# Moving lags of a causal convolution between VectorE and TensorE around the first layer norm

## The reference, cut to what matters

```
x = x + conv(x, cond)             # causal, per channel, 32 taps: y[b,t,c] = sum_j cond[31-j,c] * x[b,t-j,c]
ada = cond @ ada_w + ada_b        # shift1, scale1, gate1, shift2, scale2, gate2, one row per batch
x1  = ln(x) * (1 + scale1) + shift1
qkv = x1 @ qkv_w + qkv_b          # 16 heads of 128; attention inside each batch of 32 tokens
y   = x + gate1 * (softmax(q k / sqrt(128)) v @ out_w + out_b)
x2  = ln(y) * (1 + scale2) + shift2
out = x + (y + gate2 * (gelu(x2 @ ffn_w1 + ffn_b1) @ ffn_w2 + ffn_b2))
```

## Time and profile before

| what | value |
|---|---|
| median of 3 runs | 314.86 us (313.95 to 314.98) |
| the profiled execution's own time | 313.68 us |
| its span | 311.9 us |
| busy: PE, DVE, ACT, POOL | 96%, 56%, 55%, 39% of the span |
| granted TensorE clock | 0.999 of full speed over the span |

### The profile page before, as it was taken

One profiled execution on the slowest core, in us unless ns is written; L12 is line 12 of the kernel. 1 busy time (PEld: TensorE's weight loads), 2 busy tenths in 40 slices (PEclk: granted clock), 3 DMA queues, 4 the chain that ended last, 5 costly groups with the idle time before them and its releaser, 6 DMA issues.

```text
span 311.9 us, 6134 instructions
## 1 busy us (share of the span) xinstructions
PE 300.7 (96%) x2604; PEld 252.0 (81%) x2604; DVE 173.3 (56%) x297; ACT 171.3 (55%) x309; POOL 120.4 (39%) x103
## 2 busy tenths in 40 slices
PE   4978999999999999999999999999999999999995
PEld 3875997878898878788887888888898888688885
DVE  3997698987865635472535554440620556555232
ACT  5752567534762745486365736644762794713901
POOL 5007819331820634072337214531911571611400
PEclk9999999999999999999999999999999999999999
DMA  7902322400250070007004300520160020000012
GB/s 245 361 11 86 112 76 65 141 0 2 72 200 0 2 259 14 0 4 269 1 2 154 117 2 2 183 89 2 39 230 2 2 67 0 3 0 0 2 67 68
DMA packets 15259, 23.00 MB, mean 74 GB/s; under 512 B 792, under 2 KB 8320, under 8 KB 15232
## 3 DMA queue, kind: packets, MB, share of 16 engines
q1 hardware_dynamic: 15184, 22.58, 21.4%
q10 hardware_dynamic: 48, 0.03, 0.0%
HBM read 21.57 MB, written 1.05 MB: 73 GB/s over the span
## 4 chain that ended last, share of the span: by engine, by line
PE 85%; DVE 9%; POOL 3%; DMA 1%; ACT 1%; issue 1%; DVEq 0%; POOLq 0%
PE bank L914 18%; PE bank L916 18%; PE bank L915 18%; PE bank L988 9%; DVE xc L536 6%; PE bank L922 5%; PE bank L923 4%; PE bank L924 4%; PE bank L972 3%; POOL wl L292 3%; PE bank L869 2%; PE bank L894 1%; DMA crow<-in_cond_dram 1%; DVE yacc L667 1%; PE bank L846 1%
## 5 line engine op out<-in xcount | busy, mean ns | idle before, releaser
L292 POOL TENSOR_TENSOR wl<-raw,wh 128x512 fp32r<-128x512 f32 x72 | 98.7, 1398 | 133.2 <-ACT wh L355 116.5
L401 ACT ACTIVATE pool<-bank,bT 128x512 f32<-128x512 f32 x56 | 38.5, 688 | 57.0 <-PE bank L916 57.0
L914 PE MATMUL bank<-x1h,wl 128*128 128x512 f32 (+1 forms) x176 | 67.6, 384 | 0.8 <-DVE x1l L605 0.4
L916 PE MATMUL bank<-x1h,wh 128*128 128x512 f32 (+1 forms) x176 | 65.2, 370 | 0.0
L915 PE MATMUL bank<-x1l,wh 128*128 128x512 f32 (+1 forms) x176 | 65.1, 370 | 0.0
L653 DVE SCALAR_TENSOR_TENSOR ol<-bank,bT,oh 128x512 fp32r<-128x512 f32 x32 | 24.0, 749 | 36.7 <-ACT oh L426 35.7
L536 DVE SCALAR_TENSOR_TENSOR xc<-x,condT,xc 128x496 f32<-128x496 f32 (+27 forms) x82 | 42.8, 592 | 0.1
L355 ACT ACTIVATE wh<-raw 128x512 fp32r<-128x512 f32 x72 | 40.9, 622 | 3.5 <-PE bank L916 3.5
L914 PEld LDWEIGHTS bank<-x1h,wl 128*128 128x128 f32 x176 | 33.2, 189 | 7.8 <-DVE x1l L605 0.8
L915 PEld LDWEIGHTS bank<-x1l,wh 128*128 128x128 f32 x176 | 33.2, 189 | 6.0 <-issue 0.7
L916 PEld LDWEIGHTS bank<-x1h,wh 128*128 128x128 f32 x176 | 33.1, 188 | 5.8
(11 more groups left out here) (114 smaller groups left out, 412.8 us busy)
## 6 DMA issues: line engine op xcount, KB each, us to landing
raw<-in_L_cond_qkv_w_dram SPq DMA_DIRECT2D x24, 512.0 KB, 5.7
raw<-in_L_cond_out_w_dram SPq DMA_DIRECT2D x8, 512.0 KB, 3.6
raw<-in_L_cond_ffn_w_dram SPq DMA_DIRECT2D x4, 512.0 KB, 5.0
adaw<-in_L_cond_ada_w_dram SPq DMA_DIRECT2D x1, 1024.0 KB, 10.7
out_dram<-pool SPq DMA_DIRECT2D x3, 256.0 KB, 2.2
pool<-in_x_dram SPq DMA_DIRECT2D x2, 256.0 KB, 3.2
adaw<-in_L_cond_ada_w_dram SPq DMA_DIRECT2D x1, 512.0 KB, 5.2
pool<-in_x_dram SPq DMA_DIRECT2D x1, 512.0 KB, 6.1
```

Source lines behind the costliest of these rows:

```text
L292: g.tensor_tensor(wl[:, cols], raw[:, cols], wh[:, cols].bitcast(F32), ALU.subtract)\
L401: a.activation((q_sb if j < GH else k_sb)[:, j % GH, :], src, ACT.Identity, bias=bias(U, j // GH, j % GH)).then_inc(s_ev, 1)
L914: pe.matmul(dst, wl[:, w_cols], a_hi, start=start, stop=False)
L916: return pe.matmul(dst, wh[:, w_cols], a_hi, start=False, stop=stop)
```

## The change

VectorE takes all 16 lags 0 to 15 for the first quarter, but of the second quarter only lag 0 at first. TensorE takes lags 16 to 31 for the whole of half 0. The second quarter's lags 8 to 15 go to TensorE (`conv(1, ...)`, 256 tokens wide, into the banks `OB`) between the steps of `norm` 0; its lags 1 to 7 go to VectorE, one lag behind `centre(0)`, two behind `var_eps(0)`, four behind `x1_low(0)`. Then `conv_sum_second_quarter` adds the bank. Half 1 gets no lag on TensorE: VectorE does all 32 (`conv(2, ...)`), and its sum goes. There are 48 diagonals instead of 36 (GpSimd 16 instead of 9, ScalarE 32 instead of 27). The transposes of half 1 move behind the convolution on TensorE, into the banks `YB`, and ScalarE's copies of them behind `x1_high(0)`. `mean(1)` moves behind the first two projection tiles, `var(1)` behind the third, `spread(1)` behind the fourth. GpSimd does low parts 4 and 5 both ahead of `rstd(1)`. The load of half 1's `x` moves behind the first three weight loads.

```
-    PE_LAGS = [[... zip(range(14, 23), range(31, 22, -1)) ...], list(range(14, 17))]
+    PE_LAGS = [[lag for pair in zip(range(16, 24), range(31, 23, -1)) for lag in pair], list(range(8, 16))]
+    DVE_LAGS = [list(range(16)), list(range(1, 8)), list(range(T))]
+    DVE_SPANS = [CHUNKS[0], CHUNKS[1], CHUNKS[2]]
...
# SyncE
-            load_x(2)
             for at, src in (... biases ...):
             for i in range(3):
                 load_qkv(0, i)
+            load_x(2)
...
# GpSimd
             g.wait_ge(s_lo, CT)
-            low_part(0, 4)
+            low_parts(0, 2)
             rstd(1)
-            low_part(0, 5)
             low_parts(0, 3)
...
# ScalarE
-            for i in range(3):
-                high_parts(0, i)
+            high_parts(0, 0)
+            diagonals(ACT_FIRST, len(BY_ACT))
+            high_parts(0, 1)
             squares(0)
+            high_parts(0, 2)
             x1_high(0)
+            (copies of half 1's x, from YB)
             high_parts(0, 3)
-            squares(1)
             evac_chunk(0)
             evac_chunk(1)
+            squares(1)
             evac_chunk(2)
+            evac_chunk(3)
             x1_high(1)
...
# VectorE
             conv(0, 0, len(DVE_LAGS[0]))
-            conv_sum(0)
-            conv_sum(1)
+            conv_sum_late_lags()
             ...
             centre(0)
+            conv(1, 0, 1)
             scale_up(0)
             var_eps(0)
+            conv(1, 1, 3)
             norm(0)
             shift(0)
             x1_low(0)
+            conv(1, 3, 7)
+            conv_sum_second_quarter()
             centre(1)
             ...
-            conv(1, 0, 1)
-            conv_sum_half1()
-            conv(1, 1, 7)
+            conv(2, 0, 5)
             softmax_front(0)
...          (the later pieces: 7-9, 9-10, 10-11, 11-18, 18-20, 20-21, 21-22, 22-29 of 29 lags
              become 5-7, 7-8, 8-9, 9-17, 17-19, 19-20, 20-21, 21-32 of 32)
# TensorE
+            conv(0, 12, len(PE_LAGS[0]))
+            modulation_turned(0)
+            mean(0)
+            conv(1, 0, 2)
+            var(0)
+            conv(1, 2, 5)
+            spread(0)
+            conv(1, 5, len(PE_LAGS[1]))
+            (transposes of half 1's x, into YB)
+            project_chunk(0, (0, 1))
+            mean(1)
+            project_chunk(0, (2,))
+            var(1)
+            project_chunk(0, (3,))
+            spread(1)
+            project_chunk(0, (4, 5))
```

More of the change, by code:

```diff
@@ L57, in cond_resid_block_kernel @@
     NORMS = CHUNKS + [(0, HT), (HT, HT)]
-    PE_LAGS = [[lag for pair in zip(range(14, 23), range(31, 22, -1)) for lag in pair], list(range(14, 17))]
-    DVE_LAGS = [[j for j in range(T) if j not in lags] for lags in PE_LAGS]
-    DIAG_LAGS = PE_LAGS[0]
+    PE_LAGS = [[lag for pair in zip(range(16, 24), range(31, 23, -1)) for lag in pair], list(range(8, 16))]
+    DIAG_LAGS = PE_LAGS[0] + PE_LAGS[1]
     ND = len(DIAG_LAGS) * CT
-    BY_ACT = [(d, ct) for d in range(len(DIAG_LAGS)) for ct in range(CT) if ct == 0 or d % 2]
-    BY_POOL = [(d, 1) for d in range(0, len(DIAG_LAGS), 2)]
-    STEPS_BEFORE = [0, CT * len(DVE_LAGS[0])]
+    DVE_LAGS = [list(range(16)), list(range(1, 8)), list(range(T))]
+    DVE_SPANS = [CHUNKS[0], CHUNKS[1], CHUNKS[2]]
+    STEPS_BEFORE = [0, CT * 16, CT * 23]
+    BY_POOL = [(d, 1) for d in range(len(DIAG_LAGS)) if d >= len(PE_LAGS[0]) or d % 2 == 0]
+    BY_ACT = [(d, ct) for d in range(len(DIAG_LAGS)) for ct in range(CT) if (d, ct) not in BY_POOL]
+    ACT_FIRST = CT * len(PE_LAGS[0]) - len(PE_LAGS[0]) // 2
     with ExitStack() as ctx:
@@ L370, in _ @@
                 a.activation(part(x0, 1, CHUNKS[n]), (OB, YB)[n][1][:, 0:256], ACT.Copy).then_inc(s_xe[1], 1)
[L371 to L375, removed]
+            diagonals(2, ACT_FIRST)
             a.wait_ge(s_adap, 1)
@@ L429, in _ @@
             squares(0)
+            high_parts(0, 2)
             x1_high(0)
+            for ct in range(CT):
+                a.wait_ge(s_xt, 3 + ct)
+                a.activation(half(x0, ct, 1), YB[ct][:, :], ACT.Copy).then_inc(s_xe[2], 1)
             high_parts(0, 3)
-            squares(1)
             evac_chunk(0)
             evac_chunk(1)
+            squares(1)
             evac_chunk(2)
+            evac_chunk(3)
             x1_high(1)
-            for j in range(3, UB):
+            for j in range(4, UB):
                 if j == UB - 1:
@@ L528, in conv @@
                     j = DVE_LAGS[n][i]
+                    span = (0, HT) if n == 0 and i == 0 else DVE_SPANS[n]
                     for ct in range(CT):
-                        xs = by_batch(half(x0, ct, n))
-                        acc = by_batch(half(xc, ct, n))
+                        xs = by_batch(part(x0, ct, span))
+                        acc = by_batch(part(xc, ct, span))
                         w = condT[:, ct, T - 1 - j:T - j]
-                        if i:
-                            v.wait_ge(s_cdve, STEPS_BEFORE[n] + CT * (i - 1 + n) + ct + 1)
+                        if n == 1 and i == 0:
+                            v.wait_ge(s_in, ct + 1)
+                        elif i:
+                            v.wait_ge(s_cdve, STEPS_BEFORE[n] + CT * (i - 1) + ct + 1)
                         m = v.scalar_tensor_tensor(out=acc[:, :, j:], in0=xs[:, :, :T - j], scalar=w,
-                                                   in1=(acc if i else xs)[:, :, j:], op0=ALU.mult, op1=ALU.add)
-                        if n == 1 and i == len(DVE_LAGS[1]) - 1:
+                                                   in1=(acc if j else xs)[:, :, j:], op0=ALU.mult, op1=ALU.add)
+                        if n == 2 and i == len(DVE_LAGS[2]) - 1:
                             m.then_inc(s_in, 1)
@@ L548, in conv_sum, with conv_sum_second_quarter @@
                     v.wait_ge(s_cpe, ct + 1)
[L549 to L553, removed]
+                    v.wait_ge(s_cdve, CT * (len(DVE_LAGS[0]) - 1) + ct + 1)
+                    acc = by_batch(half(xc, ct, 0))[:, :, j:]
+                    v.tensor_tensor(acc, acc, by_batch(YB[ct][:, :])[:, :, j:], ALU.add).then_inc(s_in, 1)
+            def conv_sum_second_quarter():
                 j = PE_LAGS[1][0]
@@ L556, in conv_sum_half1 @@
                     v.wait_ge(s_cpe, CT + ct + 1)
[L557 to L560, removed]
+                    v.wait_ge(s_cdve, STEPS_BEFORE[2] - CT + ct + 1)
+                    acc = by_batch(part(xc, ct, CHUNKS[1]))[:, :, j:]
+                    v.tensor_tensor(acc, acc, by_batch(OB[ct][:, 0:HT // 2])[:, :, j:], ALU.add).then_inc(s_in, 1)
             def centre(n):
@@ L707, in _ @@
             softmax_transpose(0)
-            conv(1, 7, 9)
+            conv(2, 5, 7)
             o_low(0, 0)
             o_low(0, 1)
-            conv(1, 9, 10)
+            conv(2, 7, 8)
             o_low(0, 2)
-            conv(1, 10, 11)
+            conv(2, 8, 9)
             o_low(0, 3)
@@ L718, in _ @@
             one_plus(2, SCALE2)
-            conv(1, 11, 18)
+            conv(2, 9, 17)
             softmax_front(1)
@@ L722, in _ @@
             softmax_transpose(1)
-            conv(1, 18, 20)
+            conv(2, 17, 19)
             o_low(1, 0)
             o_low(1, 1)
-            conv(1, 20, 21)
+            conv(2, 19, 20)
             o_low(1, 2)
-            conv(1, 21, 22)
+            conv(2, 20, 21)
             o_low(1, 3)
-            conv(1, 22, len(DVE_LAGS[1]))
+            conv(2, 21, len(DVE_LAGS[2]))
             softmax_front(2)
@@ L850, in conv @@
                 last = len(PE_LAGS[n]) - 1
+                span = ((0, HT), CHUNKS[1])[n]
                 for i in range(i0, i1):
@@ L858, in conv @@
                             pe.wait_ge(s_diag[0], BY_ACT.index((d, ct)) + 1)
-                        xs = by_batch(half(x0, ct, n))
-                        m = pe.matmul(by_batch(CONV_BANK[n][ct][:, :])[:, :, j:], diag[:, CT * d + ct, :],
+                        xs = by_batch(part(x0, ct, span))
+                        m = pe.matmul(by_batch(CONV_BANK[n][ct][:, 0:span[1]])[:, :, j:], diag[:, CT * d + ct, :],
                                       xs[:, :, :T - j], start=(i == 0), stop=(i == last))
@@ L1008, in _ @@
             pe.wait_ge(s_xe[1], 2)
-            conv(0, 0, 6)
+            conv(0, 0, 8)
+            pe.wait_ge(s_adaw[0], 16)
+            modulation(0)
+            conv(0, 8, 12)
+            pe.wait_ge(s_row[1], 16 * 5)
+            pe.transpose(PB[2][:, 0:NBIAS], rows[:, :], ident[0:NBIAS, 0:NBIAS]).then_inc(s_bt, 1)
+            conv(0, 12, len(PE_LAGS[0]))
[6 more added lines that the diff above has]
+            conv(1, 5, len(PE_LAGS[1]))
             pe.wait_ge(s_x[2], 16)
@@ L1012, in _ @@
                 for t in range(TG):
-                    m = pe.transpose(OB[ct][:, t * P:(t + 1) * P], xtok[:, TG + t, ct * P:(ct + 1) * P], ident[:, :])
+                    m = pe.transpose(YB[ct][:, t * P:(t + 1) * P], xtok[:, TG + t, ct * P:(ct + 1) * P], ident[:, :])
```

(8 more changed lines are left out.)

5 lines of the change are left out of this document (1 added, 4 removed).

## The result

| | before | after |
|---|---|---|
| median | 314.74 us (8 runs, 313.91 to 314.98) | 317.46 us (8 runs, 315.83 to 318.82) |
| span of the profiled execution | 311.9 us | 316.8 us |

The ratio is 1.0091, with a 95% interval of 1.007 to 1.0112: the change made the kernel 0.9% slower, 2.7 us. My forecast was 315.1 in a range of 313.2 to 317.0; the time lies above it. Within these eight runs of each the extremes lie 3.0 us apart instead of 1.1; but the kernel before, timed again beside the experiments (23 and 29 runs), spread over 2.6 to 2.7 us too, so a wider spread is not shown.

What follows compares the result with a forecast made beforehand. Bound: when TensorE begins the projections, what is put into its full stretch, and later gaps. Gain 1.3 us, give-back and the vanished gap net +0.25: 313.9 profiled, 315.1 us on the median, range 313.2 to 317.0.

Steps and rivals of the forecast that it cites:

- The first quarter reaches the norm earlier: Convolution ahead of the first norm: VectorE ends at 18.9, TensorE at 18.5, mean(0) starts at 19.75, 3.3 us earlier.
- The filling of the first norm: First norm's waits: TensorE's filling free, VectorE's steps and low parts delay each other; first projection at 30.0, gain 1.3 us.
- The faster rival: First norm: the fills hold nobody, norm 1.1 to 2.1 us sooner than forecast, median say 313.5 us; chance 0.27.
- the one with late diagonals: Ahead of the first norm: VectorE's row holds GpSimd off, seven diagonals come late, norm 1 us later, 316.2 us; chance 0.10.
- What is given back: First projections, second quarter's norm: mean(1) adds 0.9 us, new waits follow, third chunk of tiles at 41.95, 0.75 us later.
- a row of steps holds GpSimd off to its end: VectorE beside GpSimd: a low part begun inside an unbroken row lasts 3.19 us instead of 1.3, until after the row.
- the turns: Lags 4 to 7: low parts 4 and 5 each cost VectorE 1.25 us, mean(1) waits 3.0, 317.3 us; chance 0.14.
- The gap of 0.5 us at the start of unit 1: Start of unit 1: TensorE's wait for GpSimd's low part, about 0.5 us, goes because the low part ends by 50.9.
- What costs nothing: Half 1 and unit 1: VectorE's extra lags, ScalarE's later copies and the later load of x are covered, at no cost.
- VectorE's longer half 1: Half 1: three more lags, 1.65 us against 2.05 idle ahead of unit 1's scores, 2.4 us against 5.66 later; covered.

Runs made afterwards that it cites:

- e8: Changed kernel with GpSimd's low parts 3, 4 and 5 behind the second quarter's sum, low parts 6 and 7 left in place; 314.67 us, ratio 1.0003.
- e6: As e5, with GpSimd's low part 3 also behind the second quarter's sum; 314.94 us, ratio 1.0023 to the kernel before.
- e7: As e6, with lag 16 of half 0 moved to VectorE for the first quarter, to TensorE's norm waits for the second; 315.04 us, ratio 1.0016.
- e9: As e8, with lag 16 of half 0 out of TensorE's part ahead of the norm, as in e7; 314.40 us, ratio 0.999.
- e1: Changed kernel with GpSimd's low parts 4 and 5 waiting for the second quarter's sum; 315.15 us, ratio 1.001 to the kernel before.
- the repeat: The changed kernel timed and profiled again without any edit; 317.36 us, ratio 1.008 to the kernel before.
- e5: As e1, with low parts 6 and 7 also moved behind the memset and x1_low(1); 316.09 us, ratio 1.0032 to the kernel before.
- e4: Kernel before with half 1's lags 14 to 16 moved from TensorE to VectorE, its steps cut into pieces, its sum gone; 318.13 us, ratio 1.0108.
- e10: As e4, with six matmuls of the same widths that nobody reads where TensorE did those lags; 314.32 us, ratio 0.9988 to the kernel before.
- e3: Changed kernel with five extra matmuls of 256 columns ahead of mean(1), into a bank later overwritten; 318.53 us, ratio 1.0117 to the kernel before.

## Why the prediction was wrong, by its own steps

**The first quarter reaches the norm earlier: right for VectorE, mis-sized at TensorE's end.** VectorE's last step was on time (its last ends at 18.8; I had 18.9). TensorE's end was not 18.5 but 19.5 in one profile and 20.9 in the other: I started from the end in one profile and took the removed columns off at 1.8 ns each, the price of the last pieces, while the first pieces run at about half that speed until a moment that differs. `mean(0)` came at 20.12 and 21.48, not at 19.75; 19.62 and 19.71 were reached in e8 and e6. So of the 3.3 us of gain the changed kernel had 3.0 in one profile and 1.6 in the other. Before, VectorE ended last (22.4) and hid this; now TensorE is last and shows it. This and the clock behind the wait are what differs between its two profiles; the spreads of e7 and e9, which give TensorE less there, are narrower than those of e6 and e8 (1.2 against 3.1, 0.7 against 1.9 us).

**The filling of the first norm: right in size, wrong in manner.** `conv(1, 0, 1)` lasted 2.15 us (2.4 forecast), `var_eps` came at 24.84 (24.7), `norm(0)` at 27.42 (27.6), the first projection at 29.79 (30.0). But `rstd` was not held to the end of the four steps: it took 0.88 instead of 0.72. Low part 3 held the fourth step instead (four steps took 2.59 us, not 1.5). Two errors cancelled: that the first projection came within 0.2 us of the forecast is luck. The faster rival asked for a lead above 2.2 us at `norm`, and it was 1.5; the one with late diagonals did not come either, since the 16 diagonals ended at 11.70. They were made beside an unbroken row of steps from 7.95 on, so there too the row did not hold GpSimd off to its end.

**What is given back: the step that failed.** I said that "a row of steps holds GpSimd off to its end", and had `mean(1)` wait 0.5. In the run GpSimd got in behind the first step, the steps took 4.97 us instead of 2.9, and the wait was 2.37. e1 takes the meeting away, and both go (2.89 and 0.28). My base was one meeting; against it stood three in the earlier trace rows. I had the turns as a rival with its place and price (2.5 us, 317.3 on the median), gave it 0.14, and it is what happened, at 2.1 us. That its 317.3 lies so near to the 317.46 is partly luck. In the repeat the second quarter's first tile is 3.2 us behind my 41.95, 2.1 of it by the turns and 1.15 by the first projection's late start (31.15 against 30.0); in the first profile it is 4.3 us behind, 2.1 by the turns, 2.5 by the fallen clock, less 0.2. The Trainium skill (SBUF — State Buffer, Who interferes with whom) has the rule by which it goes: two SBUF inputs on VectorE against a GpSimd instruction that reads SBUF, one whole instruction at a time. The low parts' meetings in the changed kernel (4.97 us instead of 2.89) and in e5 (9.21 instead of 5.05) follow it. Why the meeting of the earlier trace rows did not, no run here shows; it stays open.

The other terms held. From `mean(1)` to the second quarter's first tile I had 8.55 us, and at full clock it was 8.52 (36.66 to 45.18). The wait there was 0.32 (0.5 forecast). The gap of 0.5 us at the start of unit 1 went, as forecast; but from the second quarter's first tile to the end it is only 0.2 us shorter than before in one profile and 0.4 in the other, so not all of it was won.

**What costs nothing: right, for a reason I had not seen.** TensorE's filling I costed at nothing, as if it might be left out. e4 and e10 show that in the kernel before it was worth 3.4 to 3.8 us, and that matmuls which compute nothing do the same: it kept the clock. VectorE's longer half 1 was covered, as forecast.

**The missing rival.** The clock fell behind the wait of 2.4 us in one of the two profiles of the changed kernel and cost 2.5 us there; in the other it did not. It was on no list of mine. Its share of the median is small, some 0.1 us by the 14 executions.

## What to carry to other kernels

Before work is put into one engine's waits, look for what it shares with a neighbour: eight steps that took 2.89 us by themselves took 4.97 beside two of GpSimd's low parts, and a single wait on GpSimd's side gave 2.3 us back. Weigh such meetings by their number: one row that goes the other way is not a rule. When such a meeting is moved, look at what the delayed engine will meet next, as in e5. And an engine's idle-looking filler can be load-bearing: before it is taken out, ask what the clock does without it.

## What was not expected of the hardware

- Taking six matmuls (3.3 us of busy time) out of TensorE's waits in a stretch of 8.9 us, which left waits of 0.84 to 1.53 us in it, brought its granted clock there from 1.00 to 0.60, in the next stretch of 4.2 us to 0.63. The kernel took 3.4 us longer (1.9 us by 41.2 in the profile); matmuls without a reader in their place gave 3.8 us back.
- The first 32 matmul instructions of one and the same program took 8.2 and 9.6 us in two executions, and 7.3 us in e8, whose program has the same ones; the granted clock was printed as 1.00 each time.
- TensorE waited 2.17 us once in e3 with no releaser in the profile, and 1.62 us once in e4 (193.78 us); none of the other profiles has a wait of TensorE without releaser over 0.3 us behind 56 us. What causes it is open.
